# The down projection of a quantized gated MLP as a seven-product Strassen scheme

## Chip, cores and metric

One NeuronCore of a Trainium2 chip. The metric is the device time of one launch in microseconds (us). Engines: TensorE (PE), VectorE (DVE), ScalarE (ACT), GpSimd (POOL) and SyncE (SP), each with its own in-order queue; they meet at semaphores.

## What is computed

A cross attention block with layer norm and residual, then a gated MLP on 2048 tokens (16 x 128) of width 1024, inner width 2752. The MLP weights are 4-bit values with a scale and a zero for each group of 64:

```
Wg, Wu, Wd = dequantize(gate), dequantize(up), dequantize(down)   # (w - zero) * scale
x = x + xattn(layernorm(x), ctx)
h = silu(layernorm(x) @ Wg.T) * (layernorm(x) @ Wu.T)             # 2048 x 2752
out = x + h @ Wd.T                                                # 2048 x 1024
```

## The kernel before

Every product of the MLP runs in split precision: each operand is a 16-bit high part and a 16-bit low part, and a product is high x high + high x low + low x high, three matmuls of 128 x 128 by 512 columns for one term.

The inner width is cut into 10 pairs of 256 (`PAIRS`) and a rest. The 2048 tokens are two groups g of 1024. For each pair there are four gate and up **instances**, n = 4p to 4p+3, two for each half e of the pair (`idx` 0 to 3, e = idx // 2, g = idx % 2). An instance is a Strassen product (2 x 2 blocks: gate and up by two token halves) with seven block products of 12 matmuls each (`product`, L505), always in the order P1 (`s_p1`), P6, a second product into P1's bank (`s_c11`), P7, P5, P4, P3. They fill three PSUM banks a, b and c; ACT copies a to SBUF (`m1_copy`), DVE makes sums of banks and that copy (`u1_out`, `u2_out`, `c22_out`, `c21_out`, `c12_out`), ACT applies Silu (`silu0`, `silu1`), DVE multiplies (`h0_out`, `h1_out`), ACT and DVE split h into high and low (`hi0`, `hi1`, `lo0`, `lo1`). Odd and even instances use different sets of three banks (0 to 2 and 3 to 5); banks 6 and 7 are the down product's.

The **down product** is plain: for each pair 16 token tiles x 2 output halves of 6 matmuls (`down_tile`, L561), put behind products of the instances (`first_tiles`, `middle_tiles`, `last_tiles`: of the 28 places behind a product in a pair, 16 have a tile). ACT scales each result into `stage` (`evict`, L820), and POOL issues a DMA for each tile that adds it to `out` in memory (`add_tile`, L382).

The weights of a job (gate and up of e = 0, of e = 1, or down) are unpacked on DVE: `nibbles` (L1108, L1109), `minus_zero` (L1113), `times_scale` (L1118), `lo_of` (L1123), for gate and up also the four Strassen sums (`first_sums`, `second_sums`, L1132 to L1141). ACT casts the high parts. A hand-written order puts these as `work(at)` between the steps of an instance. SP loads `raw`, `raw_d` and `grid`, each when its buffer has been read.

In the attention stage before it, POOL makes sums of blocks of the normalized x (`blocks_of_x`, L358), and the last eight blocks (`LATE`) are transposed by PE inside instances 0 and 1. Behind the last pair come two more instances (40 and 41), blocks for the rest of the width (`y_block`, L651), and the last down tiles (`last_down`, L668), which DVE adds to tiles of `out` that SP has loaded back (`add_last`, L1422).

## Time and profile before

| | us |
|---|---|
| median of 3 runs (lowest 1472.64, highest 1473.21) | 1472.84 |
| the profiled execution: its own time | 1472.75 |
| the profiled execution: span, first to last instruction | 1470.9 |
| PE busy | 1453.8 (99%) |
| DVE busy | 819.7 (56%) |
| ACT busy | 635.9 (43%) |
| POOL busy | 206.6 (14%) |

Busy time is the union of an engine's instructions. Matmuls overlap: one lasts 379 ns in the rows, and the next begins before it has ended, so the pace is read from the starts of groups and the mean of one says nothing on it. A row of the timeline is one or several merged instructions of a line; in brackets stands how long the engine sat idle before it and for whom it waited. A result of PE reaches its reader when the row of its group ends, 0.20 us into the next group.

### The profile page before, as it was taken

To read this page: it belongs to the slowest core of one execution; us is meant where nothing else is said; L and a number is where in the kernel's file an instruction comes from. 1 tells how busy PE (TensorE), PEld (TensorE's weight loads), DVE (VectorE), ACT (ScalarE), POOL (GpSimd) and SP (SyncE) were. 2 spreads that over 40 slices of the span, in tenths; PEclk is the share of its full clock that TensorE was granted. 3 is DMA by queue.
4 is the path that set the end of the run, shared out by engine and by line. 5 is a ranking of instruction groups with operands and counts; after the bars stand their busy time and mean duration, and the time that the engine had idled before them with its cause. 6 is when DMAs were issued, how large, how long until landed. Compare 5 with 4: busy or idle time off the path is not lost.

```text
span 1470.9 us, 18688 instructions
## 1 busy us (share of the span) xinstructions
PE 1453.8 (99%) x6774; PEld 716.2 (49%) x6774; DVE 819.7 (56%) x1175; ACT 635.9 (43%) x1189; POOL 206.6 (14%) x265
## 2 busy tenths in 40 slices
PE   8999999999999999999999999999999999999998
PEld 6777764444444444444444444444444444444443
DVE  5898977735734644644544544553553554463365
ACT  6889883334334334243343333433424433433320
POOL 1242321011011011011011111101101101101100
PEclk9999999999999999999999999999999999999999
DMA  5322222277377467558547638638637737737794
GB/s 160 120 83 87 90 86 58 48 153 142 59 137 142 78 113 146 97 88 165 103 71 171 114 57 181 119 46 169 122 60 157 130 57 152 135 58 155 135 336 172
DMA packets 47028, 174.82 MB, mean 119 GB/s; under 512 B 6672, under 2 KB 9488, under 8 KB 42640
## 3 DMA queue, kind: packets, MB, share of 16 engines
q0 software_dynamic: 23040, 83.90, 35.0%
q1 hardware_dynamic: 23808, 90.20, 20.3%
q8 instruction: 20, 0.33, 0.1%
q10 hardware_dynamic: 144, 0.26, 0.0%
q14 instruction: 16, 0.13, 0.0%
HBM read 73.67 MB, written 100.66 MB: 119 GB/s over the span
## 4 chain that ended last, share of the span: by engine, by line
PE 93%; DVE 3%; ACT 3%; issue 1%; POOL 0%; DVEq 0%; POOLq 0%
PE ps L505 51%; PE ps L561 28%; PE ps L467 3%; PE ps L434 3%; PE ps L668 2%; PE ps L651 2%; PE ps L422 1%; PE ps L462 1%; PE ps L456 1%; ACT temps L706 1%; ACT temps L720 1%; DVE neg_max L1044 0%; PE ps L410 0%; PE ps L412 0%; ACT xt L713 0%
## 5 line engine op out<-in xcount | busy, mean ns | idle before, releaser
L505 PE MATMUL ps<-xt,w_gu 128*128 128x512 f16 x3528 | 789.0, 379 | 0.0
L505 PEld LDWEIGHTS ps<-xt,w_gu 128*128 128x128 f16 x3528 | 345.1, 98 | 414.9 <-issue 0.6
L561 PE MATMUL ps<-w_d_all,h_all 128*128 128x512 f16 x1920 | 440.5, 379 | 0.0
L820 ACT ACTIVATE stage<-ps,pow 128x512 f32<-128x512 f32 x320 | 219.8, 687 | 413.8 <-PE ps L561 413.8
L561 PEld LDWEIGHTS ps<-w_d_all,h_all 128*128 128x128 f16 (+1 forms) x1920 | 187.8, 98 | 226.6
L382 POOL DMA_DIRECT2D out<-stage x160 | 138.6, 866 | 1029.5 <-ACT stage L820 1029.5
L1187 DVE TENSOR_TENSOR temps<-ps,temps 128x512 f32<-128x512 f32 x42 | 29.0, 691 | 211.0 <-PE ps L505 211.0
L807 ACT CAST h_all<-temps 128x512 f16<-128x512 f32 x42 | 25.8, 613 | 131.0 <-DVE temps L1206 131.0
L1192 DVE TENSOR_TENSOR temps<-ps,temps 128x512 f32<-128x512 f32 x42 | 29.0, 691 | 95.1 <-PE ps L505 95.1
L1196 DVE TENSOR_TENSOR temps<-ps,temps 128x512 f32<-128x512 f32 x42 | 28.9, 689 | 75.8 <-PE ps L505 75.8
L1200 DVE TENSOR_TENSOR temps<-ps,temps 128x512 f32<-128x512 f32 x42 | 28.9, 688 | 75.2 <-PE ps L505 75.2
L1183 DVE TENSOR_TENSOR temps<-ps,temps 128x512 f32<-128x512 f32 x42 | 29.0, 691 | 71.2 <-PE ps L505 71.2
L706 ACT ACTIVATE temps<-ps,neg_max 128x256 f32<-128x256 f32 x128 | 59.3, 486 | 8.5 <-DVE neg_max L1044 8.2
L467 PE MATMUL ps<-temps,w_gu 128*128 128x512 f32 x128 | 60.2, 593 | 0.7 <-ACT temps L701 0.7
L720 ACT ACTIVATE temps<-temps,inv_total 128x256 f32<-128x256 f32 x128 | 54.7, 505 | 6.9 <-DVE inv_total L1059 6.8
L1123 DVE TENSOR_TENSOR w_gu<-quant,w_gu 128x512 f16<-128x512 f32 (+1 forms) x43 | 41.3, 961 | 26.8 <-ACT w_gu L769 26.8
L795 ACT ACTIVATE temps<-ps,pow 128x512 f32<-128x512 f32 x42 | 28.8, 687 | 61.4 <-PE ps L505 61.2
L800 ACT ACTIVATE temps<-temps,pow 128x512 f32<-128x512 f32 x42 | 30.3, 721 | 54.5 <-DVE temps L1200 54.5
L1123 DVE TENSOR_TENSOR w_gu<-raw,w_gu 128x1024 f16<-128x1024 f32 (+1 forms) x43 | 52.9, 1230 | 0.0
L434 PE MATMUL ps<-w_gu,h_all 128*128 128x256 f32 x176 | 42.7, 387 | 1.1 <-ACT w_gu L691 0.5
L1118 DVE SCALAR_TENSOR_TENSOR quant<-quant,pow,grid 128x1024 f32<-128x1024 f32 (+1 forms) x34 | 43.5, 1279 | 0.1
L1049 DVE TENSOR_TENSOR xt<-ps,xt 128x512 f16<-128x512 f32 x56 | 36.9, 679 | 11.7 <-ACT xt L713 11.5
(114 smaller groups left out, 1284.5 us busy)
## 6 DMA issues: line engine op xcount, KB each, us to landing
out<-stage POOLq DMA_DIRECT2D x160, 512.0 KB, 5.3
grid<-grids SPq DMA_DIRECT2D x136, 256.0 KB, 4.9
raw<-packed SPq DMA_DIRECT2D x22, 512.0 KB, 3.6
out<-stage SPq DMA_DIRECT2D x17, 512.0 KB, 2.9
stage<-x SPq DMA_DIRECT2D x13, 512.0 KB, 3.5
raw_d<-packed SPq DMA_DIRECT2D x12, 512.0 KB, 7.9
xt<-out SPq DMA_DIRECT2D x12, 512.0 KB, 10.4
out<-xt SPq DMA_DIRECT2D x12, 512.0 KB, 2.6
```

Of the source, the lines that this page charges most:

```text
L382: pool.dma_start(out[t, :, :], stage[:, t % STAGES, :], accum_op=ALU.add).then_inc(s_acc[t % STAGES], 16)
L434: mm = pe.matmul(ps_e[f][:, t, :], xn[b % XNS][:, cols], kk[:, par, :], start=True, stop=True)
L467: mm = pe.matmul(ps_o, v_t[:, par, h, :], prob_t[:, f, h, :], start=False, stop=(h == 1))
L505: mm = pe.matmul(bank, w_gu[e][:, wp, w, P * j:P * j + P], xt[:, xb, xp, j, cols], start=(fresh and n == 0), stop=(n == 3 * J - 1), skip_g ...
L561: mm = pe.matmul(ps[:, 6 + oh, :], h, w, start=(n == 0), stop=(n == len(products) - 1))
L706: ex = act.activation(prob[:, NTH * f + t, :], ps_e[f][:, t, :], ACT.Exp, bias=neg_max[:, f, t:t + 1], accum_out=total[:, f, t:t + 1])
L720: pn = act.activation(pr, pr, ACT.Copy, scale=inv_total[:, f, t:t + 1])
L800: act.activation(u1[:, idx % 2, :], u1[:, idx % 2, :], ACT.Silu, scale=pow2[:, 8:9]).then_inc(s_silu1, 1)
L820: act.activation(stage[:, t % STAGES, NOUT * oh:NOUT * oh + NOUT], ps[:, 6 + oh, :], ACT.Copy, scale=pow2[:, 10:11]).then_inc(s_stage, 1)
L1049: dve.tensor_tensor(xt[:, u, 1, :, P * k:P * k + P], ring_bank(("block", unit)).rearrange("p (j r) -> p j r", j=J), xt[:, u, 0, :, P * k:P ...
L1118: dve.scalar_tensor_tensor(out=t[:, cols], in0=t[:, cols], scalar=pow2[:, power:power + 1], in1=grid[:, 0, cols], op0=ALU.mult, op1=ALU.mu ...
L1123: dve.tensor_tensor(dst, src, hi, ALU.subtract).then_inc(s_weight_lo, 1)
```

## The change

The down product becomes a Strassen product too. For each pair and each token group g (a **group**, 20 in all) the blocks are: two token halves of h by the two halves e of the pair, and the two halves e of the weights by two output halves. Seven products of h blocks and weight blocks (`A11` ... `S4H` with `B11` ... `T2D`), 3 matmuls each, for each of 4 token tiles k: 84 matmuls for a group.

- **Order.** Instances are ordered token group by token group: n = 4p (e 0, g 0), 4p+1 (e 1, g 0), 4p+2 (e 0, g 1), 4p+3 (e 1, g 1). An even and an odd **tile** (as the new code calls an instance) make the h of one group; its down products run in the gaps of the next two instances (`down_gap`, at = 1 to 6 behind products 2 to 7 of the even tile, at = 7 to 10 behind the first four of the odd one).
- **PSUM.** All instances use banks 0 to 2. Down uses 3 and 4 (a chain of four products p1, p6, p7, p4 accumulates in one bank, read by ACT after each), 5 and 6, and 7.
- **h sums.** POOL makes four sums of h blocks for a group (`last_sum`, then `first_sums` when `h1` of the odd tile is there). ACT and DVE split seven blocks (`h_block_hi`, `h_block_lo`) where they split four.
- **Results.** ACT reads the chain's bank four times for each k, DVE adds the other bank with a multiply and add (`add_to`) three times for each k.
- **Weights.** Down weights get four sums and seven blocks. `raw_d` is gone: all jobs share `raw`. e = 1 of gate and up is needed one instance earlier, and its last steps sit in tile 4p.
- **DMAs that add.** Three for each k (two of 256 KB, one of 512 KB) in place of two of 512 KB for two tiles.
- The rest of the width is handled as before, in other buffers (`hx`, `hy`, `w_last`); SP waits for all adds before it loads `out` back.

The diff below is cut; in the `work` functions of DVE at its end only the new lines stand.

```diff
@@ -36,6 +36,11 @@
+A11, S3H, A12, S2H, S1H, A22, S4H = range(7)
+B11, B21, B22, T1D, T3D, T4D, T2D = range(7)
...
-        raw_d = sb("raw_d", [P, JW], I32)
...
+        park = sb("park", [P, 7168], F32)
+        more = sb("more", [P, NOUT], F32)
...
+        part12 = [stage[:, 0, NOUT:N], stage[:, 1, NOUT:N], more[:, :], stage[:, 0, NOUT:N]]
+        m1s, u2, s3h, s1h = (temps[:, k // 2, k % 2, :] for k in range(4))
+        act_h, u1 = temps[:, 2, :, :], temps[:, 3, :, :]
+        h_hi = park[:, 0:1792].bitcast(F16).rearrange("p (k t) -> p k t", k=7)
+        h_lo = park[:, 1792:3584].bitcast(BF16).rearrange("p (k t) -> p k t", k=7)
+        w_d = park[:, 3584:7168].bitcast(F16).rearrange("p (a k o) -> p a k o", a=2, k=7)
...
+            with sp.Fori(2, 3 * PAIRS + 2, 1) as j:
+                load_grid(j, 2 * j)
+                load_raw(j, 4 * j)
             load_grid(3 * PAIRS + 2, 6 * PAIRS + 4)
+            load_raw(3 * PAIRS + 2, 12 * PAIRS + 6)
+            load_grid(3 * PAIRS + 3, 6 * PAIRS + 5)
...
@@ -377,14 +391,64 @@
-            def add_tile(d, t):
-                pool.wait_ge(s_stage, 2 * d + 2)
-                pool.dma_start(out[t, :, :], stage[:, t % STAGES, :], accum_op=ALU.add).then_inc(s_acc[t % STAGES], 16)
+            def last_sum(group):
+                n = 4 * (group // 2) + 2 * (group % 2)
+                pool.wait_ge(s_h0, n + 1)
+                pool.wait_ge(s_h1, n + 1)
+                wait(pool, s_h_lo, 7 * (group - 1) + S2H + 1)
+                pool.tensor_tensor(s3h, act_h[:, 0, :], u1[:, 0, :], ALU.subtract).then_inc(s_h_sum, 1)
+            def first_sums(group):
+                n = 4 * (group // 2) + 2 * (group % 2) + 1
+                pool.wait_ge(s_h1, n + 1)
+                pool.wait_ge(s_h_lo, 7 * group + S3H + 1)
+                pool.tensor_tensor(s3h, u1[:, 1, :], s3h, ALU.subtract).then_inc(s_h_sum, 1)
+                pool.tensor_tensor(s1h, u1[:, 0, :], u1[:, 1, :], ALU.add).then_inc(s_h_sum, 1)
+                pool.wait_ge(s_h_sum, 4 * group + 2)
+                pool.wait_ge(s_h_lo, 7 * group + A12 + 1)
+                pool.tensor_tensor(act_h[:, 1, :], act_h[:, 1, :], s3h, ALU.subtract).then_inc(s_h_sum, 1)
...
+            def adds(group, at):
+                k = (at - 1) // 2
+                if at % 2:
+                    if k < QUADS:
+                        add11(QUADS * group + k)
+                elif k >= 1:
+                    add2(QUADS * group + k - 1)
+                    add12(QUADS * group + k - 1)
...
-            for d in range(B * PAIRS):
-                add_tile(d, d % B)
+            last_sum(0)
+            for group in range(2 * PAIRS):
+                first_sums(group)
+                for at in range(1, 8):
+                    adds(group, at)
+                if group + 1 < 2 * PAIRS:
+                    last_sum(group + 1)
+                for at in range(8, 11):
+                    adds(group, at)
...
@@ -507,140 +571,161 @@
-                a, b, c = (ps[:, 3 * (idx % 2) + k, :] for k in range(3))
+            def instance(n, e, g, lo, after):
...
-            def down_tile(p, g, t, terms):
+            def down_product(bank, h, w, k, fresh):
+                rows = slice(P * k, P * k + P)
+                pe.matmul(bank, h_hi[:, h, rows], w_d[:, 0, w, :], start=fresh, stop=False, skip_group_check=not fresh)
+                pe.matmul(bank, h_hi[:, h, rows], w_d[:, 1, w, :], start=False, stop=False, skip_group_check=not fresh)
+                return pe.matmul(bank, h_lo[:, h, rows], w_d[:, 0, w, :], start=False, stop=True,
+                                 skip_group_check=not fresh)
...
+                def p1(k):
+                    h_ready(k, A11)
+                    w_ready(k, 1)
+                    wait(pe, s_out21, 4 * group + k - 1)
+                    down_product(ps[:, 3 + k % 2, :], A11, B11, k, True).then_inc(s_down1, 1)
+                def p2(k):
+                    h_ready(k, A12)
+                    w_ready(k, 2)
+                    wait(pe, s_out11, 4 * group + k)
+                    down_product(ps[:, 7, :], A12, B21, k, True).then_inc(s_down2, 1)
+                def p6(k):
+                    h_ready(k, S2H)
+                    w_ready(k, 4)
+                    pe.wait_ge(s_r1, 4 * group + k + 1)
+                    down_product(ps[:, 3 + k % 2, :], S2H, T2D, k, False).then_inc(s_down6, 1)
+                def p5(k):
+                    h_ready(k, S1H)
+                    wait(pe, s_out12, 4 * group + k - 1)
+                    down_product(ps[:, 5 + k % 2, :], S1H, T1D, k, True).then_inc(s_down5, 1)
+                def p7(k):
+                    pe.wait_ge(s_r6, 4 * group + k + 1)
+                    down_product(ps[:, 3 + k % 2, :], S3H, T3D, k, False).then_inc(s_down7, 1)
+                def p4(k):
+                    h_ready(k, A22)
+                    pe.wait_ge(s_r7, 4 * group + k + 1)
+                    down_product(ps[:, 3 + k % 2, :], A22, T4D, k, False).then_inc(s_down4, 1)
+                def p3(k):
+                    h_ready(k, S4H)
+                    pe.wait_ge(s_out22, 4 * group + k + 1)
+                    down_product(ps[:, 5 + k % 2, :], S4H, B22, k, False).then_inc(s_down3, 1)
+                k = (at - 1) // 2
+                if at % 2:
+                    if k >= 1:
+                        p7(k - 1)
+                    if k < QUADS:
+                        p1(k)
+                        p2(k)
+                else:
+                    if k < QUADS:
+                        p6(k)
+                        p5(k)
+                    if k >= 1:
+                        p4(k - 1)
+                        p3(k - 1)
...
+            def h_block_hi(group, block):
+                else:
+                    act.wait_ge(s_h_sum, 4 * group + {S3H: 1, S2H: 2, S1H: 3, S4H: 4}[block])
+                    src = {S3H: s3h, S1H: s1h, S2H: s3h, S4H: act_h[:, 1, :]}[block]
+                used = {A11: s_down1, S3H: s_down7, A12: s_down2, A22: s_down4, S1H: s_down5, S2H: s_down6,
+                        S4H: s_down3}[block]
+                wait(act, used, QUADS * group)
+                act.copy(h_hi[:, block, :], src).then_inc(s_h_hi, 1)
...
+            def down_gap(group, at):
...
+                k = (at - 1) // 2
+                d = QUADS * group
+                if at % 2:
+                    if k >= 1:
+                        act.wait_ge(s_down7, d + k)
+                        row_free(s_add2, k - 1)
+                        scaled(stage[:, 2 + (k - 1) % 2, NOUT:N], 3 + (k - 1) % 2).then_inc(s_r7, 1)
+                    if k < QUADS:
+                        act.wait_ge(s_down1, d + k + 1)
+                        row_free(s_add11, k)
+                        scaled(stage[:, k % 2, 0:NOUT], 3 + k % 2).then_inc(s_r1, 1)
+                else:
+                    if k < QUADS:
+                        act.wait_ge(s_down6, d + k + 1)
+                        if k != 3:
+                            wait(act, s_add12[(k + 3) % QUADS if k == 0 else k], 16 * group)
+                        else:
+                            act.wait_ge(s_add12[0], 16 * group + 16)
+                        scaled(part12[k], 3 + k % 2).then_inc(s_r6, 1)
+                    if k >= 1:
+                        act.wait_ge(s_down4, d + k)
+                        scaled(stage[:, 2 + (k - 1) % 2, 0:NOUT], 3 + (k - 1) % 2).then_inc(s_out21, 1)
...
+            def even_tile(n, group, before, lo, work):
+                before()
+                m1_copy(n)
+                if group is not None:
+                    down_gap(group, 1)
+                work(0)
+                if group is not None:
+                    for block in (S2H, S1H, A22, S4H):
+                        h_block_hi(group, block)
+                work(1)
+                silu0(n, 0, lo)
+                for at in range(2, 7):
+                    if group is not None:
+                        down_gap(group, at)
+                    work(at)
...
+            def down_sums(j):
+                dve.wait_ge(s_weight_lo, 4 * j + 1)
+                dve.tensor_tensor(q0, q1, q0, ALU.subtract).then_inc(s_comb, 1)
+                dve.wait_ge(s_comb, 4 * j + 1)
+                dve.tensor_tensor(q1, r1, q1, ALU.subtract).then_inc(s_comb, 1)
+                dve.wait_ge(s_weight_lo, 4 * j + 2)
+                dve.wait_ge(s_comb, 4 * j + 2)
+                dve.tensor_tensor(r1, r1, q0, ALU.subtract).then_inc(s_comb, 1)
+                dve.wait_ge(s_comb, 4 * j + 3)
+                dve.tensor_tensor(r0_, r0_, r1, ALU.subtract).then_inc(s_comb, 1)
...
+            def h_block_lo(group, block):
+                src = {A11: act_h[:, 0, :], S3H: s3h, A12: act_h[:, 1, :], A22: u1[:, 1, :], S1H: s1h, S2H: s3h,
+                       S4H: act_h[:, 1, :]}[block]
+                dve.wait_ge(s_h_hi, 7 * group + block + 1)
+                dve.tensor_tensor(h_lo[:, block, :], src, h_hi[:, block, :], ALU.subtract).then_inc(s_h_lo, 1)
+            def add_to(part, bank):
+                return dve.scalar_tensor_tensor(out=part, in0=ps[:, bank, :], scalar=pow2[:, 10:11], in1=part,
+                                                op0=ALU.mult, op1=ALU.add)
+            def down_gap(group, at):
+                k = (at - 1) // 2
+                d = QUADS * group
+                if at % 2:
+                    if k >= 1:
+                        dve.wait_ge(s_down5, d + k)
+                        dve.wait_ge(s_r7, d + k)
+                        add_to(stage[:, 2 + (k - 1) % 2, NOUT:N], 5 + (k - 1) % 2).then_inc(s_out22, 1)
+                    if k < QUADS:
+                        dve.wait_ge(s_down2, d + k + 1)
+                        dve.wait_ge(s_r1, d + k + 1)
+                        add_to(stage[:, k % 2, 0:NOUT], 7).then_inc(s_out11, 1)
+                elif k >= 1:
+                    dve.wait_ge(s_down3, d + k)
+                    dve.wait_ge(s_r6, d + k)
+                    add_to(part12[k - 1], 5 + (k - 1) % 2).then_inc(s_out12, 1)
...
+            def even_tile(n, group, before, sums, work):
+                before()
+                work(0)
+                if group is not None:
+                    h_block_lo(group, S2H)
+                    h_block_lo(group, S1H)
+                u1_out(n, 0, sums)
+                if group is not None:
+                    down_gap(group, 1)
+                    h_block_lo(group, A22)
+                    h_block_lo(group, S4H)
+                work(1)
+                work(2)
+                u2_out(n)
+                if group is not None:
+                    down_gap(group, 3)
+                work(3)
+                c22_out(n)
+                if group is not None:
+                    down_gap(group, 4)
+                work(4)
+                c21_out(n)
+                h0_out(n, 0)
+                if group is not None:
+                    down_gap(group, 5)
+                work(5)
+                c12_out(n, 0)
+                if group is not None:
+                    down_gap(group, 6)
+                work(6)
+            def odd_tile(n, group, own, before, sums, work):
+                before()
+                if group is not None:
+                    down_gap(group, 7)
+                work(0)
+                u1_out(n, 1, sums)
+                if group is not None:
+                    down_gap(group, 8)
+                work(1)
+                h_block_lo(own, A11)
+                if group is not None:
+                    down_gap(group, 9)
+                work(2)
+                u2_out(n)
+                if group is not None:
+                    down_gap(group, 10)
+                work(3)
+                c22_out(n)
+                work(4)
+                c21_out(n)
+                h0_out(n, 1)
+                h_block_lo(own, S3H)
+                work(5)
+                c12_out(n, 1)
+                h_block_lo(own, A12)
+                work(6)
...
             def second_up(p):
                 def work(at):
+                    if at == 0:
+                        job_scale(3 * p + 1, 6)
                     if at == 1:
+                        plain_lo(1, 12 * p + 4)
                     if at == 3:
+                        first_sums(12 * p + 4, 12 * p + 4)
+                    if at == 4:
+                        second_sums(12 * p + 4)
                     if at == 5:
+                        mixed_lo(1, 12 * p + 4)
                 return work
+            def down_weights(p):
                 def work(at):
                     if at == 0:
+                        job_nibbles(3 * p + 2)
                     if at == 1:
+                        job_minus(3 * p + 2)
                     if at == 2:
+                        times_scale(q, 6 * p + 5, 7)
                     if at == 3:
+                        times_scale(r, 6 * p + 6, 7)
                     if at == 4:
+                        down_plain_lo(3 * p + 2)
+                        down_sums(3 * p + 2)
+                    if at == 6:
+                        down_mixed_lo(3 * p + 2, 0)
+                return work
+            def next_weights(p):
+                def work(at):
+                    if at == 0:
+                        down_mixed_lo(3 * p + 2, 1)
+                    if at == 3:
+                        job_nibbles(3 * p + 3)
+                    if at == 4:
+                        job_minus(3 * p + 3)
                     if at == 5:
+                        job_scale(3 * p + 3, 6)
                 return work
             def next_up(p):
                 def work(at):
+                    if at == 0:
+                        plain_lo(0, 12 * p + 12)
+                        first_sums(12 * p + 12, 12 * p + 12)
                     if at == 1:
+                        second_sums(12 * p + 12)
                     if at == 2:
+                        mixed_lo(0, 12 * p + 12)
                     if at == 5:
+                        job_nibbles(3 * p + 4)
+                    if at == 6:
+                        job_minus(3 * p + 4)
                 return work
...
```

## Rows read from the trace of the kernel before

**Rows 1.** The page: busy us, share and instructions of each engine.

```profile
PE 1453.8 (99%) x6774; PEld 716.2 (49%) x6774; DVE 819.7 (56%) x1175; ACT 635.9 (43%) x1189; POOL 206.6 (14%) x265
```

**Rows 2.** Windows from:to, us; then busy of each engine, clock, DMA share, GB/s.

```profile
0.00:20.00 20.00, 13.61 (x61) 12.27 (x62) 10.41 (x26) 7.91 (x25) 2.99 (x14) 0.93 0.58 197
222.87:1403.47 1180.60, 1179.61 (x5482) 536.70 (x5480) 599.76 (x761) 441.85 (x640) 144.34 (x166) 1.00 0.59 114
```

**Rows 3.** The chain that ended last: start, us, what; two pieces one pair apart.

```profile
828.65 28.49 PE ps L505 x132
...
942.61 28.49 PE ps L505 x132
```

**Rows 4.** Groups by line and shape: count, busy us, mean ns, idle and releaser.

```profile
L505 PE MATMUL ps<-xt,w_gu 128*128 128x512 f16 x3528 | 789.0, 379 | 0.0
L561 PE MATMUL ps<-w_d_all,h_all 128*128 128x512 f16 x1920 | 440.5, 379 | 0.0
L820 ACT ACTIVATE stage<-ps,pow 128x512 f32<-128x512 f32 x320 | 219.8, 687 | 413.8 <-PE ps L561 413.8
...
L807 ACT CAST h_all<-temps 128x512 f16<-128x512 f32 x42 | 25.8, 613 | 131.0 <-DVE temps L1206 131.0
```

**Rows 5.** Timeline of DVE, a stretch inside one pair, with starts to read paces.

```profile
717.32 0.69 DVE L1196 TENSOR_TENSOR temps<-ps,temps 128x512 f32<-128x512 f32 x1 [2.22 <-PE ps L505]
718.04 0.75 DVE L1206 SCALAR_TENSOR_TENSOR temps<-temps,pow 128x512 f32<-128x512 f32 x1
718.71 1.28 DVE L1118 SCALAR_TENSOR_TENSOR quant<-quant,pow,grid 128x1024 f32<-128x1024 f32 x1
719.91 0.69 DVE L1200 TENSOR_TENSOR temps<-ps,temps 128x512 f32<-128x512 f32 x1
720.52 0.68 DVE L1219 TENSOR_TENSOR h_all<-temps,h_all 128x512 bf16<-128x512 f32 x1
...
726.30 1.22 DVE L1123 TENSOR_TENSOR w_d_all<-quant,w_d_all 128x1024 f16<-128x1024 f32 x1
727.43 1.22 DVE L1123 TENSOR_TENSOR w_d_all<-raw_d,w_d_all 128x1024 f16<-128x1024 f32 x1
```

**Rows 6.** Timeline of DVE, the start of a weight job in the same pair.

```profile
730.88 0.68 DVE L1108 TENSOR_SCALAR quant<-raw 128x1024 int32<-128x1024 int32 x1
731.48 0.69 DVE L1109 TENSOR_SCALAR raw<-raw 128x1024 int32<-128x1024 int32 x1
...
733.47 1.21 DVE L1113 TENSOR_TENSOR quant<-quant,grid 128x1024 f32<-128x1024 int32 x1
734.60 1.22 DVE L1113 TENSOR_TENSOR raw<-raw,grid 128x1024 f32<-128x1024 int32 x1
```

**Rows 7.** Timeline of POOL, block sums of the attention stage from idle.

```profile
48.38 1.51 POOL L358 TENSOR_TENSOR w_d_all<-h_all 128x512 f32<-128x512 f32 x1 [1.00 <-DVE h_all L1036]
50.04 1.30 POOL L358 TENSOR_TENSOR w_d_all<-h_all,w_d_all 128x512 f32<-128x512 f32 x1
```

**Rows 8.** Timeline of POOL, the same sums with weight work on DVE.

```profile
156.97 1.04 POOL L358 TENSOR_TENSOR w_d_all<-h_all 128x512 f32<-128x512 f32 x1
157.97 1.74 POOL L358 TENSOR_TENSOR w_d_all<-h_all,w_d_all 128x512 f32<-128x512 f32 x1
```

**Rows 9.** Timeline of DVE in the same stretch.

```profile
157.22 1.34 DVE L1123 TENSOR_TENSOR w_gu<-quant,w_gu 128x512 f16<-128x512 f32 x1
158.48 2.31 DVE L1123 TENSOR_TENSOR w_gu<-raw,w_gu 128x1024 f16<-128x1024 f32 x1
```

**Rows 10.** Timeline of all engines, the first instances: a late block awaited, then POOL.

```profile
230.13 1.04 POOL L358 TENSOR_TENSOR w_d_all<-h_all 128x512 f32<-128x512 f32 x1
...
244.82 0.63 PE L456 MATMUL ps<-ident,w_d_all 128*128 128x128 f32 x4 [0.99 <-DVE xt L1049]
```

**Rows 11.** Issues of DMAs: count, KB each, median us from issue to landing.

```profile
out<-stage POOLq DMA_DIRECT2D x160, 512.0 KB, 5.3
...
raw<-packed SPq DMA_DIRECT2D x22, 512.0 KB, 3.6
```

More of the change, by code:

```diff
@@ L823, in instance @@
[L823 to L842 removed]
+                act.activation(u1[:, e, :], u1[:, e, :], ACT.Silu, scale=pow2[:, 8:9]).then_inc(s_silu1, 1)
@@ L952, in y_silu @@
+            hx_block_hi(2)
             def y_silu(at):
```

732 lines of the change are left out of this document (343 added, 389 removed).

## The prediction

> **What bounds the kernel now.** I read the page's busy times first: PE is busy 99% of the span, DVE 56%, ACT 43%, POOL 14% [rows 1]. The window over all gate, up and down work, 1180.60 us long, says the same, at full granted clock [rows 2], and the chain that ended last is PE's own matmuls: two equal pieces of it, one pair apart, start 113.96 us apart [rows 3]. A pair has 4 x 84 + 192 = 528 matmuls, so one takes 113.96 / 528 = 0.2158 us, as inside the piece (28.49 / 132). A product of 12 takes 2.59 us. So PE never waits in the pairs; less PE work is less time, as long as the others keep up.
>
> **What is removed on PE.** Down goes from 1920 matmuls [rows 4] to 20 groups x 84 = 1680. The window of 1180.60 us holds 3528 + 1920 matmuls (1175.8), eight late transposed blocks of about 0.44 (3.5, a transposed block's row is 0.6 long and the next product overlaps it [rows 10]), and 1.2 of waits, 0.99 of them one wait for a late block [rows 10]. With 5208 matmuls and no wait it would be 1127.5: 53 us less. This is the floor, 1472.75 - 53 = 1419.7 in the profiled execution's own time, which stands 0.09 under the median.
>
> **What is added elsewhere, by sums.** DVE, a pair: 24 multiply-and-adds from PSUM, 6 more low halves of h, four weight sums and one and a half more weight halves: 24 x 0.75 + 6 x 0.68 + 4 x 0.69 + 1.9 = 27 us [rows 5]. It had 599.76 / 1180.6 x 114 = 58 [rows 2]; 85 of 109 us is 78%. ACT keeps its 32 evictions [rows 4], and gets 6 casts of 0.61 and 1.7 of weights. POOL gets 8 sums of 1.0 to 1.5 [rows 7, 8] and 8 more issues. None is full. SP: the shared `raw` comes 3.6 us after its issue [rows 11]; by the order of the queues the tightest job (last step of one job in the odd tile 4p+3 at 18, `nibbles` at 24) has 6. Stage buffers come free 5.3 us after an issue [rows 11], and are wanted again after some 10. Both cost nothing; were a landing to take twice as long, still nothing. Smaller DMAs move the same bytes. The end is taken as unchanged: the last adds land at about the end of tile 41, where SP waited anyway.
>
> **What ends last now: the head of an even tile.** I lay the queues out from the start of P1 = 0. P6 is at 2.59, gap 1 at 5.18 (6 matmuls), the third product at 6.47, gap 2 at 9.06 (p6 then p5 of k = 0, 0.65 each), P7 at 10.36. Gap 2 wants the low halves of S2H and S1H, P7 wants `u1`, which stands behind both on DVE. A low half needs ACT's cast, which needs POOL's sum, which needs `h1` of the tile before. All this is new; before, no sum stood between h and down.
>
> When does `h1` end? Paces on DVE are start to start [rows 5, 6]: 0.60 for a half (0.61 behind a sum), 0.67 for a multiply-add, 1.13 for a weight half of 1024, 1.20 for a scale, 0.72 for an operation that needs the one ahead. Nibbles follow at 0.60 and minus-zero at 1.13 [rows 6].
> - Tile 4p: in the odd tile ahead P4's result comes at -2.39. Behind it c21 0.72, h0 0.67, low S3H 0.60, nibbles 1.20, c12 0.61, low A12 0.60, minus-zero 2.27: `h1` starts at 4.28, POOL can go at 5.05, the next DVE operation (a scale) at 4.95.
> - Tile 4p+2: P5's result at -4.98, then c22 0.61, down halves 0.60 + 1.13, four sums 2.88, c21 0.72, h0 0.67, low S3H 0.60, c12 0.61, low A12 0.60, mixed half 1.13: `h1` at 4.57, POOL at 5.3, the next DVE operation (mixed half) at 5.24.
>
> If POOL ran free: from idle 1.5, then 1.0 [rows 7, 8], so S1H is there at 7.6 to 7.9; cast 0.61, low half 0.7, `u1` 0.7: 9.6 to 9.9, ahead of 10.36. No stall.
>
> **But POOL does not run free.** A low half on DVE took 1.34 in place of 0.68, and one of 1024 took 2.31 in place of 1.22, when POOL was in a sum; POOL's sum took 1.74 in place of 1.30 [rows 5, 7 to 9]. Read in time they take turns: DVE's first ends at 158.56, which less its own 0.68 is a start at 157.88 where POOL's sum ends; POOL's second then runs, DVE's next ends at 160.79, less 1.22 is 159.57. A turn of POOL is 0.9 (one tensor read, 157.88 - 156.97) or 1.1 (two tensors, 159.57 less DVE's read end 158.48). DVE operations with one operand in PSUM beside POOL kept their length. Weight work, h products and h halves have both operands in SBUF. In the new order POOL's three sums of `first_sums` fall on exactly those.
>
> The Trainium skill ("SBUF — State Buffer", Who interferes with whom) says that a DVE instruction with two SBUF inputs and a GpSimd instruction that reads SBUF block each other for a whole instruction. With 1.30 for every turn of POOL instead of the rows' 0.9 and 1.1, the stalls below would grow by about 1.6 a pair and the time by some 16 us.
>
> The turns, with 1.1 for S2H and S4H (two tensors) and 0.9 for S1H:
> - Tile 4p: scale to 6.15, S2H 7.25, scale 8.45, S1H 9.35, low S2H 9.95, S4H 11.05 (it asks 0.4 after S1H, while low S1H still waits 0.65 for its cast), low S1H 11.65 and 0.08 more. p5 starts at 11.75, P7 at 12.4, not 10.36: **2.05** lost. At 0.9 for all 1.65, at 1.1 for all 2.25.
> - Tile 4p+2: mixed half to 6.37, S2H 7.47, S1H 8.4, low S2H 9.0, S4H 10.1, low S1H 10.7. p5 at 10.8, P7 at 11.45: **1.1**. Bounds 0.7 and 1.3.
> - Further on in the tile u2, c22 and c21 have 2 us or more left, so a stall is neither made up nor passed on.
> Sum 3.15 a pair, 9 pairs: 28.4. Tile 40 has scales of half size: 1.0. Bounds 2.35 to 3.55: 22 to 33.
>
> **The first three tiles** have no down work to cover DVE, one set of banks, and e = 1 one tile early. Laid out the same way: minus-zero in tile 0 alternates with POOL's block sums (they run past 230 [rows 10]), so late block 1 is late and with it the bank of block 2: 2.4. In tile 1 DVE does a whole down job; c21 comes about 2 us after P6 of tile 2 could start, and that tile's head loses 3 more: 7.4. Bounds 5 and 9. A wait on DVE for `raw` is possible here; it counts in the bound.
>
> **Sum.** 1472.75 - 53 + 28.4 + 1.0 + 7.4 = 1456.6; I forecast **1457** (own range 1447 to 1467).
>
> **Rivals.**
> 1. *The collisions don't decide.* If low S1H on DVE goes ahead of S4H (the two ask within about 0.2 us of each other), or `h1` comes 1 us earlier, the heads lose nothing. For it: the margin is small. Against it: the two heads have the same pattern, and rows 8 and 9 show POOL taking each turn it asked for. 1472.75 - 53 + 5 of start = **1425**. Chance 0.20. Between the two (one head of the two stalls): 1440, 0.07.
> 2. *Slower: POOL's turns are long.* From idle a sum took 1.51 [rows 7]. If each new sum, which waits for something each time, holds DVE off for 1.5, a pair loses 3.4 + 2.5 = 5.9: 53 for nine pairs, 2 for tile 40, and 10 at the start: 1472.75 - 53 + 65 = **1485**. It decides from about 4.9 a pair on, that is POOL turns of 1.3 us. Against it: sums in line took 0.9 to 1.1 beside DVE [rows 8, 9]. Chance 0.09.
> 3. *The change doesn't do what it says:* 240 matmuls fewer are certain from the code; but a 3-matmul product with its waits might not follow at pace. All 6-matmul tiles did (12 matmuls in 2.59). If 560 down products cost 0.02 each, +11: 1468. Chance 0.05, half of it within 0.2% of before.
> 4. *The clock falls.* The window shows 1.00 through a late-block wait, and the first 20 us, where PE is idle a third, 0.93 [rows 2]. Stalls of 2 us in 30 leave PE far busier than that. If a tenth of the pairs' 1100 us ran at 1.2 GHz, half speed, +55: 1512. Chance 0.02. The Trainium skill ("TensorE: Matmul & The Clock Gate", A second HAM failure mode) tells of a kernel whose clock went up and down from short idle times between bank groups; no run here shows that.
>
> **Chances and range.** Forecast 0.57, rivals 0.20, 0.07, 0.09, 0.05, 0.02. The range takes in rival 1 and the forecast with its bounds and leaves out the slow ones: 1423 to 1470. What a measurement of this kernel can tell from no change is about 0.2%, 2.9 us: faster 0.57 + 0.20 + 0.07 + 0.02 = 0.86, within 0.2% 0.03, slower 0.11.
>
> **What would show it.** In the trace after: PE pieces one pair apart start about 111.9 us apart (108.8 if rival 1 holds, 114.7 for rival 2); PE's idle time is in front of down matmuls p6 and p5 in gap 2 of even tiles, ended by DVE's low halves; DVE's scale and half rows beside POOL's sums are about 1 us longer than alone; PE's idle in odd tiles is nil. The step is wrong if those DVE rows keep their lengths, if PE waits elsewhere (p7 for ACT's eviction r6, P4 for u2), or if the matmul pace is above 0.216.

## The result, and the profile after

| | before | after |
|---|---|---|
| median of 20 runs each, us | 1473.13 (1472.64 to 1474.21) | 1476.10 (1473.49 to 1479.43) |
| profiled execution, us: own time, span | 1472.75, 1470.9 | 1475.23, 1473.4 |
| first tile to y blocks, us | 1180.60 | 1179.59 (222.55 to 1402.14) |

The ratio is 1.0020 with a 95% interval of 1.0013 to 1.0026: about 3 us slower, just at the bound of what can be told from no change. 1457 was forecast, with a range that ended at 1470. The 240 matmuls are gone, 52 us at their pace; but PE is idle for 58.7 us of the span where it was for 17.1.

The page of the kernel after: busy times, then groups of its section 5 (line engine op, out<-in, count | busy, mean ns | idle time before, releaser).

```profile
PE 1414.7 (96%) x6534; PEld 690.0 (47%) x6534; DVE 1119.2 (76%) x1535; ACT 678.6 (46%) x1269; POOL 421.3 (29%) x425
...
L607 PE MATMUL ps<-park 128*128 128x512 f16 x560 | 212.8, 380 | 35.7 <-DVE park L1396 35.7
...
L1396 DVE TENSOR_TENSOR park<-temps,park 128x512 bf16<-128x512 f32 x140 | 125.7, 909 | 20.9 <-ACT park L915 18.1
...
L407 POOL TENSOR_TENSOR temps<-temps 128x512 f32<-128x512 f32 x20 | 43.6, 2180 | 217.4 <-DVE temps L1389 217.4
```

Against [rows 1, 4]: PE 39 us less busy in a span 2.5 us longer. All of the idle time shown ahead of down's matmuls stands before the first of a product (L607) and is ended by DVE's low halves (L1396). A low half takes 909 ns in the mean; before it took 680. A POOL sum of `h` (L407, S2H) takes 2180 ns where one beside nothing took 1.30 us [rows 7].

The chain that ended last, two pieces one pair apart as in [rows 3]:

```profile
658.66 5.20 PE ps L569 x24
...
771.68 5.19 PE ps L569 x24
```

This pair takes 113.02 us. Its 504 matmuls at 0.2158 are 108.77, so 4.25 are lost; 3.15 were forecast. Eight of the nine pairs of the loop take 112.8 to 113.1, so 4.2 are lost in the mean; the ninth takes 114.75 and is taken up below under the clock. Here is the head of one tile 4p, whose P1 starts at 666.26. Timelines (start, us, engine line operation, [idle before <-releaser]) of DVE, POOL and PE:

```profile
666.63 0.69 DVE L1249 TENSOR_SCALAR quant<-raw 128x1024 int32<-128x1024 int32 x1 [0.67 <-DMA raw<-packed]
...
671.30 0.75 DVE L1389 SCALAR_TENSOR_TENSOR temps<-temps,pow 128x512 f32<-128x512 f32 x1
671.97 1.28 DVE L1259 SCALAR_TENSOR_TENSOR quant<-quant,pow,grid 128x1024 f32<-128x1024 f32 x1
673.16 2.30 DVE L1259 SCALAR_TENSOR_TENSOR raw<-raw,pow,grid 128x1024 f32<-128x1024 f32 x1
675.38 3.42 DVE L1396 TENSOR_TENSOR park<-temps,park 128x512 bf16<-128x512 f32 x2
678.73 0.68 DVE L1359 TENSOR_TENSOR temps<-ps,temps 128x512 f32<-128x512 f32 x1
```
```profile
672.14 2.24 POOL L407 TENSOR_TENSOR temps<-temps 128x512 f32<-128x512 f32 x1 [9.76 <-DVE temps L1389]
674.34 2.24 POOL L408 TENSOR_TENSOR temps<-temps 128x512 f32<-128x512 f32 x1
676.54 1.71 POOL L411 TENSOR_TENSOR temps<-temps 128x512 f32<-128x512 f32 x1
```
```profile
677.26 0.39 PE L607 MATMUL ps<-park 128*128 128x512 f16 x1 [1.76 <-DVE park L1396]
...
678.86 0.39 PE L607 MATMUL ps<-park 128*128 128x512 f16 x1 [0.78 <-DVE park L1396]
...
679.52 2.75 PE L569 MATMUL ps<-xt,w_gu 128*128 128x512 f16 x12
```

The pattern is the forecast one: the second scale on DVE is 1.02 us longer than the first, the two halves 2.14 longer than two alone (1.28), and POOL's three sums stand between them. P7 should start 10.36 us after P1, at 676.62, and starts at 679.52: 2.9 lost. In tile 4p+2 (P1 at 723.55) P7 starts at 735.25, not 733.90: 1.35.

### The profile page after: what moved, and what is told of

It is laid out like the page before. It is cut to its first block, busy times and chain, and to the rows that moved or that the text cites. A ratio compares the mean times of both kernels' runs of the same rounds, so it can differ in the third digit from the quotient of the medians.

```text
span 1473.4 us, 19706 instructions
## 1 busy us (share of the span) xinstructions
PE 1414.7 (96%) x6534; PEld 690.0 (47%) x6534; DVE 1119.2 (76%) x1535; ACT 678.6 (46%) x1269; POOL 421.3 (29%) x425
## 4 chain that ended last, share of the span: by engine, by line
PE 70%; DVE 10%; issue 10%; POOL 5%; ACT 4%; DMA 0%; SPq 0%; DVEq 0%; POOLq 0%
PE ps L569 35%; PE ps L607 8%; PE ps L609 7%; PE ps L608 7%; DVE park L1396 3%; POOL temps L407 3%; PE ps L531 3%; PE ps L498 3%; POOL temps L408 2%; PE ps L756 2%; PE ps L486 1%; PE ps L526 1%; PE ps L520 1%; DVE park L1264 1%; DVE temps L1373 1%
## 5 line engine op out<-in xcount | busy, mean ns | idle before, releaser
L1399 DVE SCALAR_TENSOR_TENSOR stage<-ps,pow,stage 128x512 f32<-128x512 f32 x220 | 159.5, 747 | 156.0 <-ACT stage L918 87.3
L607 PE MATMUL ps<-park 128*128 128x512 f16 x560 | 212.8, 380 | 35.7 <-DVE park L1396 35.7
L609 PE MATMUL ps<-park 128*128 128x512 f16 x560 | 212.6, 380 | 0.0
L608 PE MATMUL ps<-park 128*128 128x512 f16 x560 | 212.5, 379 | 0.0
L429 POOL DMA_DIRECT2D out<-stage x80 | 69.4, 867 | 288.8 <-ACT stage L918 288.8
L416 POOL DMA_DIRECT2D out<-stage x80 | 70.6, 883 | 276.0 <-DVE stage L1399 276.0
L1396 DVE TENSOR_TENSOR park<-temps,park 128x512 bf16<-128x512 f32 x140 | 125.7, 909 | 20.9 <-ACT park L915 18.1
L915 ACT CAST park<-temps 128x512 f16<-128x512 f32 x140 | 84.2, 615 | 124.2 <-DVE temps L1383 69.9
L607 PEld LDWEIGHTS ps<-park 128*128 128x128 f16 x560 | 54.7, 98 | 116.6 <-DVE park L1396 28.1
L407 POOL TENSOR_TENSOR temps<-temps 128x512 f32<-128x512 f32 x20 | 43.6, 2180 | 217.4 <-DVE temps L1389 217.4
L609 PEld LDWEIGHTS ps<-park 128*128 128x128 bf16 x560 | 54.8, 98 | 66.3 <-issue 0.3
L608 PEld LDWEIGHTS ps<-park 128*128 128x128 f16 x560 | 54.8, 98 | 61.4
L422 POOL DMA_DIRECT2D out<-stage x60 | 68.4, 1140 | 12.1 <-DVE stage L1399 12.1
L498 PE MATMUL ps<-w_gu,park 128*128 128x256 f32 x256 | 62.4, 388 | 1.1 <-ACT w_gu L779 0.5
L498 PEld LDWEIGHTS ps<-w_gu,park 128*128 128x128 f32 x256 | 47.6, 193 | 11.7 <-issue 5.3
```

Source lines behind the costliest of these rows:

```text
L407: pool.tensor_tensor(s3h, u1[:, 1, :], s3h, ALU.subtract).then_inc(s_h_sum, 1)
L416: pool.dma_start(out[t, :, 0:NOUT], stage[:, d % 2, 0:NOUT], accum_op=ALU.add).then_inc(s_add11[d % 2], 16)
L498: mm = pe.matmul(ps_e[f][:, t, :], xn[b % XNS][:, cols], kk[:, par, :], start=True, stop=True)
L607: pe.matmul(bank, h_hi[:, h, rows], w_d[:, 0, w, :], start=fresh, stop=False, skip_group_check=not fresh)
L608: pe.matmul(bank, h_hi[:, h, rows], w_d[:, 1, w, :], start=False, stop=False, skip_group_check=not fresh)
L609: return pe.matmul(bank, h_lo[:, h, rows], w_d[:, 0, w, :], start=False, stop=True, skip_group_check=not fresh)
```

## The experiments

All times are medians, with the ratio to the kernel before and its 95% interval. Each kernel is the changed one with the edit shown; all compute the whole output. The pair is the mean of the nine pairs of the loop.

| | us | ratio | pair, us |
|---|---|---|---|
| three sums on DVE | 1461.4 | 0.992 (0.991 to 0.994) | 111.8 |
| the same, ACT's casts later | 1449.0 | 0.984 (0.982 to 0.985) | 110.4 |
| S4H late | 1468.9 | 0.997 (0.996 to 0.998) | 112.9 |
| h1 first in 4p | 1451.3 | 0.986 (0.984 to 0.987) | 110.7 |
| h1 first in 4p, S4H late | 1441.1 | 0.978 (0.977 to 0.980) | 109.8 |
| h1 first in 4p and 4p+2 | 1453.6 | 0.986 (0.984 to 0.988) | 110.8 |
| all together | 1434.5 | 0.974 (0.972 to 0.975) | 109.8 |

**Are the turns the cause, or DVE's load?** The sums go to DVE.

```
-  (POOL, first_sums)  S2H, S1H, S4H
+  (DVE, even_tile, behind h1_out)  s3h = u1[1] - s3h;  s1h = u1[0] + u1[1]
+  (DVE, ahead of the low halves of A22 and S4H)  act_h[1] = act_h[1] - s3h
```

> The changed kernel with the three sums S2H, S1H and S4H moved from POOL to DVE, behind h1 (S2H, S1H) and ahead of the last two low halves (S4H). Nothing else is moved. Theory (turns: what costs is that a POOL sum and a DVE operation with two SBUF inputs block each other): no DVE row is stretched any more, 1.28 for the scales and 0.68 for the halves, although DVE has three operations of 0.7 us more in each head. Laid out with the rows of the changed kernel: tile 4p has h1 at +5.0, sums to +6.5, scales to +9.6, low S2H +10.2, low S1H and u1 to +11.5, so P7 is 1.2 late in place of 2.9; tile 4p+2 has h1 at +4.5, all low halves by +9.0 and u1 by +9.7, nothing late in place of 1.35. A pair 110.0 us apart in place of 113.0, time about 1446. Rival (the chain through DVE is simply too long, turns or no turns): 2.1 us more of DVE work in each head comes on top, a pair 117 us apart, about 1511. Rival (the time is POOL's own slowness only, DVE rows beside it stay as they are): also 1446, but then DVE rows would have been at their normal length before.

It came to 1461.4. DVE, in the same head:

```profile
666.70 1.28 DVE L1253 SCALAR_TENSOR_TENSOR quant<-quant,pow,grid 128x1024 f32<-128x1024 f32 x1
667.89 1.28 DVE L1253 SCALAR_TENSOR_TENSOR raw<-raw,pow,grid 128x1024 f32<-128x1024 f32 x1
669.09 1.29 DVE L1390 TENSOR_TENSOR park<-temps,park 128x512 bf16<-128x512 f32 x2
```

All rows have their own length again, and although DVE has 2.1 us more to do in each head, the kernel is 15 us faster. That rules out plain load as the cause; and as the second scale took 2.30 beside POOL's sum and takes 1.28 here, it was not POOL's slowness alone. Tile 4p+2 loses nothing any more, as laid out. But 15 us of the 30 are missing, and PE shows where: in gap 3 p7 now waits for an eviction of ACT.

```profile
675.57 0.39 PE L601 MATMUL ps<-park 128*128 128x512 f16 x1 [1.60 <-ACT stage L912]
```

**What is late next: ACT's order.** ACT casts S4H, then two weight blocks of the up job, then does silu, and only then the eviction `r6`. As S4H came later, all of that came later. The two weight casts one step back:

```
 def second_up(p): def work(at):     # ACT
-        if at == 1:  plain_hi(6 * p + 2, 1)
+        if at == 2:  plain_hi(6 * p + 2, 1)
```

> The first of these kernels (three sums on DVE) lost 1.6 to 1.9 us a pair in gap 3 of tile 4p, where p7 waits for ACT's eviction r6: ACT has cast S4H, then the up job's first two weight blocks (0.6 + 1.0 us) and silu ahead of it. Here those two weight casts stand one step later on ACT, behind r6; the sums stay on DVE. Theory (two bounds one behind the other: turns on DVE, then the order of ACT's queue): the wait goes, a pair 110.0 us apart in place of 111.85, time 1461.4 - 9 x 1.85 - 1, about 1444 to 1446, which is what the first of these kernels was expected to give. Rival (the rest of its miss is DVE's longer queue): no change, 1461.

It came to 1449.0, a pair 110.41 us apart: 12.4 back. The wait in gap 3 is gone. 3 to 5 us more than forecast are left; 1.5 of them stand in the tail (PE waits 5.82 us there, in place of 4.30).

**One turn taken out of the way.**

```
-  pool.wait_ge(s_h_lo, 7 * group + A12 + 1)     # ahead of the S4H sum
+  pool.wait_ge(s_h_lo, 7 * group + S1H + 1)
```

> One wait changed in the changed kernel: POOL's S4H sum waits for the low half of S1H, and not only for that of A12. S4H is not needed before gap 4. Theory (turns): the turn that S4H takes between the low halves of S2H and S1H goes out of the way of S1H; in tile 4p P7 starts 1.0 us earlier, in 4p+2 about as much, a pair 111.0 us apart, with tiles 2 and 40 about 1456. Rival (no turns, the chain of h1, sum, cast, half decides): S4H is not on that chain, so nothing moves, 1476.

1468.9: 7 us, not 20. In tile 4p the second wait in gap 2 did go, and P7 came 0.9 earlier, as laid out; and then ACT's queue took that back and more, 1.5, in gap 3 of the same tile (PE, then ACT):

```profile
674.53 0.39 PE L607 MATMUL ps<-park 128*128 128x512 f16 x1 [1.71 <-DVE park L1396]
...
679.98 0.39 PE L607 MATMUL ps<-park 128*128 128x512 f16 x1 [1.29 <-ACT stage L918]
```
```profile
676.67 0.62 ACT L915 CAST park<-temps 128x512 f16<-128x512 f32 x1 [1.66 <-POOL temps L411]
677.20 0.61 ACT L850 CAST w_gu<-quant 128x512 f16<-128x512 f32 x1
677.72 1.04 ACT L852 CAST w_gu<-raw 128x1024 f16<-128x1024 f32 x1
678.67 0.68 ACT L894 ACTIVATE temps<-ps,pow 128x512 f32<-128x512 f32 x1
679.25 0.68 ACT L918 ACTIVATE stage<-ps,pow 128x512 f32<-128x512 f32 x1
```

Tile 4p+2 did come 0.85 shorter, and tile 4p about as much longer, so a pair hardly moved. Of the 5.9 us between the two profiled executions 2.4 stand in the first four tiles and 0.9 in tile 40; of the 2.6 of the nine pairs 1.8 are the one pair with a lower clock in the changed kernel's execution. So this run does not show that the turn of S4H costs 1 us in each tile; the run with both edits, below, shows it for tile 4p+2.

**h1 ahead of the weight work in tile 4p.**

```
 (DVE) next_up, step 6:      - job_minus
 (DVE) second_up, step 0:    - job_scale         + minus_zero(q)
 (DVE) second_up, step 1:    - plain_lo          + minus_zero(r), job_scale
 (DVE) second_up, step 2:                        + plain_lo
 (ACT) second_up:            - step 1: plain_hi  + step 2: plain_hi
 (DVE) y_weights of tile 40 likewise
```

> Order on DVE in tile 4p only (and in tile 40): the two minus-zero operations of the up job, which stood ahead of h1, go behind it, one of them and both scales behind the low halves and u1; ACT's two casts of that job go one step later with them. Same work, same sums on POOL. Theory: h1 starts at +3.1 in place of +5.0, POOL's three turns then fall beside one minus-zero and gaps, low S2H at +7.8 and low S1H at +9.6, u1 +10.3: the 2.9 us of tile 4p go to 0 to 0.3, the 1.35 of tile 4p+2 stay. A pair 110.2 to 110.5 us apart, time 1450 (1447 to 1454). Rival (DVE has too much in this tile wherever it stands): the stall comes back later in tile 4p or at the start of tile 4p+1, as a wait of P4 for u2 or of P1 for the weights, and the pair stays at 113.

1451.3, a pair 110.67 us apart. The same work, the same sums on POOL. POOL's first sum still loses a turn to a minus-zero, the other two run at 1.25 and 1.27, and PE has no wait in gap 2 of tile 4p:

```profile
663.15 2.17 POOL L407 TENSOR_TENSOR temps<-temps 128x512 f32<-128x512 f32 x1 [6.68 <-DVE temps L1389]
665.30 1.25 POOL L408 TENSOR_TENSOR temps<-temps 128x512 f32<-128x512 f32 x1
666.52 1.27 POOL L411 TENSOR_TENSOR temps<-temps 128x512 f32<-128x512 f32 x1
```

**The later S4H on top of it**, where ACT no longer stands in the way:

> The new order of tile 4p (h1 first) and the later S4H sum together. In tile 4p nothing waits any more, so there S4H changes nothing; in tile 4p+2 its turn goes out of the way of low S1H: that half comes at 733.65 in place of 734.5 of the changed kernel's trace, P7 0.85 us earlier. No weight cast of ACT stands in front of r6 in tile 4p+2, so the 1.3 us that the later S4H lost to it in tile 4p do not come back. A pair 109.8 us apart in place of 110.67, with tile 2 about 1451.3 - 8.5 = 1443. Rival (the gain of the later S4H is always given back to ACT): 1451.

1441.1, a pair 109.82. One turn of POOL less in tile 4p+2 is worth the 0.85 us laid out. The S4H sum now stands beside DVE operations that read PSUM (L1359, L1399), which keep their 0.68 and 0.74 us, and itself takes 1.27.

**h1 first in tile 4p+2 too**: one half of the down weights' low parts, which stood ahead of h1, goes behind it.

```
 def down_weights: -  step 6: down_mixed_lo(3 * p + 2, 0)
 def next_weights: +  step 0: down_mixed_lo(3 * p + 2, 0)   # ahead of half 1
```

> The new order of tile 4p, and in tile 4p+2 h1 ahead of both low halves of the down weights (before: one of the two behind h1), so that h1 starts 0.8 us earlier (+3.7 in place of +4.5). Theory (turns): POOL's first two sums now meet both long operations: they alternate to +8.85, low S2H +9.5, S4H's turn to +10.6, low S1H +11.2; P7 is 1.5 late in place of 1.35, so a pair 110.8 us apart, 1451 to 1453. Rival (what counts is when h1 is ready): 0.8 less in each tile 4p+2, a pair 109.9, 1444.

1453.6, a pair 110.78: nothing gained, though h1 is ready 0.8 us earlier. In exchange the S1H sum meets a long operation, and takes 2.24 us in place of 1.26. This is the sharpest of the comparisons between "when is h1 ready" and "what stands beside POOL's sums": the second decides.

**The tail.** After, the y blocks start 1.33 us earlier than in the kernel before, and the span is 2.5 us longer, so 3.8 us were lost behind. Its trace there, ACT and then PE:

```profile
1424.59 0.68 ACT L1099 ACTIVATE temps<-ps,pow 64x512 f32<-64x512 f32 x1 [3.94 <-issue]
```
```profile
1426.89 0.82 PE L756 MATMUL ps<-park,w_gu 128*128 128x512 f16 x3 [4.30 <-DVE xt L1678]
```

The silu's input was there at 1420.3. "issue" means that the engine waited for nothing the profile shows. The list of DMA queues (packets, MB, share) in a window of 1 us inside this idle time, 1422 to 1423, has a transfer of code:

```profile
q14 instruction: 1, 0.01, 2.0%
```

Eight instructions of one column put on ACT in tile 40:

> The changed kernel with eight copies of one column on ACT added in tile 40, behind the last eviction of that tile, where ACT is idle; their result is not used. They only move the code behind them by eight instructions. In the tail of the changed kernel ACT's silu of the third y block starts 3.94 us after its input was there, with no semaphore to wait for, and PE then waits 4.30 us; in that stretch the trace has a transfer of the instruction queue. Theory (ACT waits there for the next block of its code): the boundary falls eight instructions earlier in the program, beside work that nobody waits for, and the 4.30 us go: about 1472. Rival (the wait comes from something else, such as the 16 loads of rows from out in the same stretch): no change, 1476.

1471.0 (ratio 0.998, 0.998 to 0.999), and the wait is gone (PE waits 0.19 in the same place). Then waits for a semaphore that has long had its value, 8, 128 and 256 of them, which are instructions too:

> The same with one wait behind each of the eight evictions, so eight instructions more, as in the run with eight copies, by another kind of instruction. Theory: no wait in front of the silu of the third y block, about 1472. Rival (what helped was the copies' own time in tile 40): 1476.

1473.6 (1.000, 0.999 to 1.001). The wait had moved: it stood in front of a cast, two rows ahead of the silu, and PE waited 2.56. The page of this run counts three instructions more than that of the changed kernel (19709 and 19706), so the eight waits are only three of them; in the next two runs they are 64 and 128.

```profile
1422.14 0.62 ACT L1121 CAST park<-temps 64x512 f16<-64x512 f32 x1 [3.55 <-issue]
```

> The changed kernel with 128 waits added on ACT in tiles 40 and 41, sixteen behind each of eight evictions, for a semaphore that has long had its value. An instruction transfer of this queue brings 8 KB; if that is 128 instructions, the boundary of the tail comes back to where it was. Theory (ACT waits for its next block of code): unlike with eight instructions more, the wait of 3.9 us ahead of the silu of the third y block is there again, PE waits 4.3 us behind it, and the trace has one more transfer of the instruction queue; about 1476, plus what the waits themselves delay (0 to 2). Rival (any shift of ACT's work against the loads of rows makes the wait go): about 1472.

> As the kernel with 128 waits, with 32 behind each of the eight evictions. By the pages' counts of instructions the eight waits gave 3 more and the 128 waits 64 more (two waits go into one instruction); these 256 should give 128 more, a whole block of 8 KB if an instruction has 64 bytes. Eight waits (3 instructions) moved the wait for nothing visible from the silu of the third y block to the cast that stands three instructions ahead of it; 64 more made it go. Theory (a code boundary every 128 instructions): with 128 more it stands in front of the silu of the third y block again, 3.8 to 3.9 us, PE waits some 4 us behind it; 1476 plus up to 2 for the waits themselves. Rival (what helped was only the shift in time): it is gone, as with 64, about 1472.

1471.6 (0.999, 0.998 to 1.000) and 1470.9 (0.999, 0.998 to 1.000). In front of the silu the wait is gone in both. But it has moved again, and not vanished: with 128 waits ACT stands in tile 41, with 256 in tile 40, where nobody on PE waits for it.

```profile
1381.78 0.62 ACT L1059 CAST w_gu<-temps 128x512 f16<-128x512 f32 x1 [2.57 <-issue]
```
```profile
1370.08 0.62 ACT L1080 CAST w_gu<-quant 128x512 f16<-128x512 f32 x1 [3.11 <-issue]
```

In front of two other casts that stand behind 32 added waits ACT is idle for 0.55, so these are not the time of the waits themselves. So the wait belongs to a place in ACT's code and not to a time: in the changed kernel and the seven here whose ACT code is no longer than its own, PE waited 4.0 to 5.8 us there, wherever that place lay between 1392 and 1427 us; three instructions more moved it by two rows, 64 more into tile 41 and 128 more into tile 40. In each of these traces a transfer of the instruction queue starts 1.6 to 2.2 us before the operation that stood. The forecast that the wait comes back in front of the silu with 128 more fails; where the boundaries lie stays open. (With 128 waits PE still waits 2.02 us ahead of that y block; there DVE had waited 4.60 us for `raw` to land, 2.29 in the changed kernel.)

**The start.** Tile 0: low half of late block 0 ahead of the nibbles, minus-zero and scale one step later; tile 1: the down job one step earlier.

> The changed kernel with the new order of tiles 0 and 1 alone. The traces of the two kernels with h1 first and S4H late, without and with this order, differ by 1.6 us at the start of the y blocks, not by the 5.4 laid out: the late blocks' waits fell from 3.35 to 1.1, but c21 of tile 0 (1.02) and a late block in tile 1 (1.19) are awaited instead. Expected from that: 1476.1 - 1.6 = 1474.5. If the heads of tiles 2 and 4 had hidden part of it, up to 5 less, 1471.

1473.8 (1.001, 1.000 to 1.002): by the medians 2.3 of the 10 us that the start loses, but this interval overlaps that of the changed kernel. The two kernels with h1 first and S4H late, without and with this order, have the start of the y blocks 1.6 us apart, and that is the firmer number. What the order freed in one place was asked for in the next: c21 of tile 0 and a late block of tile 1 are awaited now. DVE has no room there; in the changed kernel it was idle for 0.9 us between 229 and 249.

**All that paid**, in one kernel:

> Everything that paid: h1 first in tile 4p, S4H late, the eight instructions on ACT that move the code boundary in the tail, and a new order in tiles 0 and 1: the low half of late block 0 goes ahead of the nibbles of the second job, and minus-zero and scale of that job one step later; in tile 1 the nibbles, minus-zero and scale of the down job each one step earlier. Expected: 1443 of the kernel with h1 first and S4H late, less 4.3 in the tail, less 1.75 + 1.6 for the two late blocks in tile 0 and 2.1 for the wait of P6 in tile 2 (c21 behind the down job): 1433. If the start is bound by POOL's block sums instead, late blocks wait as before and it is 1438 to 1439.

1434.5, 1.5 over what was laid out, and 39 us (2.6%) under the kernel before. Of the start's gain 1.6 of the 5.4 came. Its chain has the pairs 109.82 apart, 1.05 above what the matmuls need, half of it in tile 4p+2 and half in tile 4p+3:

```profile
645.55 12.95 PE ps L569 x60
...
755.37 12.95 PE ps L569 x60
```

## Why the prediction was wrong

Its steps, one by one. The profiled execution's time was to be 1456.6 and was 1475.2.

- *Matmul pace, floor.* Right. An odd tile of the changed kernel has 84 matmuls of its own and ten 3-matmul products; from its P1 to the next tile's are 24.61 us, which is 114 matmuls at 0.2158. So short products follow at pace, and rival 3 falls. Over the whole window the floor came out some 0.7 higher than laid out.
- *Where the stall is.* Right: gap 2 of even tiles, ended by DVE's low halves; no wait in odd tiles. DVE, busy 87 of 113 us in a pair, was not full; its order was what PE waited for.
- *Size of the stall.* Too small, and this is the term of the sum that failed first: 3.15 a pair were laid out and 4.2 came, 0.65 above the upper bound of 3.55, in nine pairs 9.4 us. Two terms. `h1` started at +5.04 in tile 4p, not +4.28, as the nibbles waited 0.67 for `raw` (ten such waits in the trace, 6.3 us). This landing was called free, with 6 us of room, by a median of 3.6 us [rows 11]. The room is 6.1 (659.87 to 665.96), the landing 6.6, in a stretch with two adding stores of stage rows (DMA view of 655 to 670; KB, us to landing):

```profile
raw<-packed SPq DMA_DIRECT2D x1, 512.0 KB, 6.6
```

  And S1H's turn is as long as the others: 1.12 (L408's end at 676.58, less 675.46 where the scale ends), where 0.9 was taken from one row. Rival 1 (no stall) and rival 2 (turns of 1.5) both fall; the time came out between forecast and rival 2 for other reasons.
- *Tile 40.* 1.8, not 1.0.
- *Start.* 10.0, not 7.4 (and its bound was 9): late blocks 1.75 + 1.60, c21 2.12, the head of tile 2 3.6 (0.6 of it at the lower clock), and 0.9 more of clock behind it. The nibbles, an operation with one operand in SBUF, were blocked by POOL too, which the layout had left free (DVE beside a POOL sum of 1.88; alone 0.69):

```profile
227.34 1.99 DVE L1250 TENSOR_SCALAR raw<-raw 128x1024 int32<-128x1024 int32 x1
```

- *The tail unchanged.* Wrong, and not in any rival: 3.8 us. A wait of 4.1 on code and 1.7 of clock came, and one of 2.06 of the same kind on DVE, at 1446 in the trace before, went (PE waited 1.65 for it).
- *Clock.* Held at nothing but as a rival of 55 us. It cost 1.6 in tile 2, 1.8 at 1018 and 1.7 in the tail, each time behind a wait of PE. A window (us; busy of PE and the rest; clock): 

```profile
1015.00:1025.00 10.00, 8.12 (x29) 3.20 (x30) 8.13 (x11) 5.72 (x9) 2.97 (x3) 0.83 0.66 131
```

  There 12 matmuls took 4.15 us (chain view) in place of 2.59, part of them at the lower level of 1.2 GHz, and the next six ran at full pace. The Trainium skill ("TensorE: Matmul & The Clock Gate", A second HAM failure mode) tells of such an up and down; in this trace it comes to 5 us in all, and that the up and down here has the cause that the page gives is not shown.

Sum of the misses: 9.4 (pairs) + 0.8 (tile 40) + 2.6 (start) + 1.8 (clock at 1018) + 3.8 (tail) + 0.7 (floor), less 0.3 for an earlier first tile, is 18.8; 18.6 were missed. So every step that had been laid out was too low by some tenths, the largest of them counted nine times, and two things, the tail and the clock, were not in the sum. With 4.2 a pair known, the time would have been called 1466: the change would still have been called a gain. What made it a loss is the tail, the start and the clock together.

The Trainium skill ("SBUF — State Buffer", Who interferes with whom) says that a DVE instruction with two SBUF inputs contends with a GpSimd instruction that reads SBUF, that the shared port pair is an exclusive lock, and, of the two-port modes, that whoever issues first has it for the whole instruction. The traces agree in kind: with an operation on both sides waiting they alternate. A DVE operation was held off 1.02 to 1.12 us by a sum that takes 1.25 to 1.30 alone, so not for all of it. By the same section a `tensor_scalar` in a two-port mode contends as well; the row of the nibbles above fits that (alone they take 0.60 from start to start, a `tensor_tensor` of the same size 1.13), and a reader of it would have had part of the start's miss.

## What to carry to other kernels

When work is taken from the engine that bounds, write down for each new operation on POOL which DVE operations stand beside it: with two operands in SBUF they alternate, about 1.05 us each way for 128x512 in f32, and a reorder that puts the sums beside idle time or beside operations that read PSUM costs nothing (here 25 us back from one such order, and 10 more from a second, with not one instruction less). After each such fix look at the next engine's queue for work that nobody waits for standing ahead of work that PE waits for. Terms that count once (start, tail) deserve the care of those that count nine times when the gain forecast is 1%.

## What the runs showed of the hardware that was not expected

- A wait of 2.6 to 3.9 us on ACT in straight-line code, with no semaphore behind it, tied to a place in the code, with a code transfer of 8 KB (0.16 MB in 20 packets on queue 14) in the same microseconds. DVE has one of 3.1 to 3.2 us in the tail of both kernels with the sums on DVE. In the loop of the changed kernel no queue has such a wait. The Trainium skill ("Runtime: NRT & Kernel Launch", Instruction fetch mechanics) calls the cost of a block boundary mostly hidden, with blocks of 16 KB; here the transfers of this queue are of 8 KB, and, if the wait is a boundary, one cost 4 us, while DMAs of rows filled the queues. That ACT waits for that transfer is the likeliest reading; shown is only that added instructions move the wait, and that it then costs PE less or nothing.
- Behind a stall of PE some microseconds at the lower clock of 1.2 GHz can follow: in two of the twenty heads of even tiles and in the tail, 1.6 to 1.8 us each time. The other eighteen heads, eight of them with stalls of the same size, kept the full clock; what tells them apart stays open.
- A load of 512 KB took 3.1 to 6.7 us to land, median 4.3, by what else was in the queues. A median is no bound for a wait that stands once in a pair.
